# A two-layer block on one core: expert weights, router, x2 and h as two fp16 parts in place of two fp32r parts, with weight scales found on chip

## The reference, cut to what matters

```
x = x + attention(layernorm(x), w_qkv, w_out)
x = x + experts(layernorm(x), Wg, Wu, Wd, Wr, temperature)

attention: 16 heads of 16, rotary q and k, q = elu(q*s)+1, k = elu(k*s)+1,
           kv += k v^T, ks += k, out_t = (q kv) / max(q ks, 1e-6), out @ w_out
experts:   gate = einsum('btd,edi->beti', x, Wg)       # E = 8, D = 256, I = 256
           up   = einsum('btd,edi->beti', x, Wu)
           h    = silu(gate) * up
           e_out = einsum('beti,eid->betd', h, Wd)
           out  = einsum('bte,betd->btd', weights, e_out)
weights:   inh = sigmoid(x @ Wr / temperature); exp(-|inh - 1/e| / 0.1) inside a zone,
           else the two nearest experts; normalised to sum 1
```

## Time and profile before

| | before |
|---|---|
| median of 3 runs | 807.97 us |
| profiled execution, span from first to last instruction | 806.5 us |
| TensorE busy | 760.2 us (94%), 6660 matmuls |
| VectorE busy | 603.2 us (75%) |
| ScalarE busy | 465.4 us (58%) |
| GpSimd busy | 484.7 us (60%) |
| mean granted TensorE clock | 0.968 of full |
| device memory read, written | 16.13 MB, 4.19 MB |

### The profile page before, as it was taken

The page is one execution under the profiler, slowest core; times in us unless marked ns, Lnnn a source line. Parts: engine busy times, 40 slices in busy tenths (PEclk is TensorE's granted clock), DMA queues, the critical chain, the costliest instruction groups (busy, mean ns, idle before and its releaser), DMA issues.

```text
span 806.5 us, 18062 instructions
## 1 busy us (share of the span) xinstructions
PE 760.2 (94%) x6660; PEld 654.1 (81%) x6660; DVE 603.2 (75%) x1596; ACT 465.4 (58%) x886; POOL 484.7 (60%) x538
## 2 busy tenths in 40 slices
PE   4475899999999999999999999999999999999997
PEld 2364688888888888888888888888888888888886
DVE  6788797878877797778877797787877787765433
ACT  3664776666566656666666556657665566534221
POOL 3785678765666665655666666566666555653232
PEclk9676799999999999999999999999999999999999
DMA  4544124122211123122101221121111121100000
GB/s 139 127 103 110 41 78 93 40 43 68 40 28 24 34 66 41 41 43 54 41 20 35 43 66 40 41 43 27 41 40 40 41 53 28 27 1 27 1 1 27
DMA packets 97319, 38.27 MB, mean 47 GB/s; under 512 B 74192, under 2 KB 96976, under 8 KB 97232
## 3 DMA queue, kind: packets, MB, share of 16 engines
q1 hardware_dynamic: 90704, 30.83, 18.1%
q10 hardware_dynamic: 6528, 6.29, 2.7%
HBM read 16.13 MB, written 4.19 MB: 25 GB/s over the span
## 4 chain that ended last, share of the span: by engine, by line
PE 88%; DVE 5%; POOL 2%; ACT 2%; issue 1%; DMA 1%; SPq 0%; DVEq 0%; ACTq 0%; POOLq 0%
PE y L446 22%; PE gate L413 22%; PE up L413 21%; PE front L288 5%; PE back L333 3%; PE front L289 3%; PE back L369 2%; PE back L344 2%; PE up L381 1%; PE front L311 1%; PE front L394 1%; PE back L326 1%; PE back L356 1%; POOL a_lo L1131 1%; PE back L311 1%
## 5 line engine op out<-in xcount | busy, mean ns | idle before, releaser
L1159 POOL TENSOR_TENSOR h_lo<-work,h_hi 128x512 fp32r<-128x512 f32 x128 | 166.3, 1299 | 66.0 <-ACT h_hi L640 66.0
L1131 POOL TENSOR_TENSOR a_lo<-am,a_hi 128x512 f16<-128x512 f32 x120 | 144.6, 1206 | 54.9 <-ACT a_hi L568 52.3
L446 PE MATMUL y<-wd_hi,h_hi 128*128 128x256 f32 x512 | 148.1, 289 | 1.7 <-DVE xa L1032 1.7
L446 PE MATMUL y<-wd_lo,h_hi 128*128 128x256 f32 x512 | 143.9, 281 | 0.0
L446 PE MATMUL y<-wd_hi,h_lo 128*128 128x256 f32 x512 | 143.8, 281 | 0.0
L1020 DVE TENSOR_TENSOR work<-work,up 128x512 f32<-128x512 f32 x128 | 87.1, 680 | 72.1 <-PE up L413 71.7
L640 ACT ACTIVATE h_hi<-work 128x512 fp32r<-128x512 f32 x128 | 80.6, 630 | 64.5 <-DVE work L1020 39.4
L1032 DVE SCALAR_TENSOR_TENSOR xa<-y,wo,xa 128x256 f32<-128x256 f32 x256 | 113.5, 470 | 4.5 <-PE y L446 4.5
L446 PEld LDWEIGHTS y<-wd_hi,h_hi 128*128 128x128 f32 x512 | 96.5, 189 | 4.9 <-issue 2.1
L446 PEld LDWEIGHTS y<-wd_lo,h_hi 128*128 128x128 f32 x512 | 96.4, 188 | 3.1
L446 PEld LDWEIGHTS y<-wd_hi,h_lo 128*128 128x128 f32 x512 | 96.4, 188 | 0.0
(11 more groups left out here) (200 smaller groups left out, 1722.2 us busy)
## 6 DMA issues: line engine op xcount, KB each, us to landing
xr<-xT SPq DMA_DIRECT2D x32, 128.0 KB, 2.5
xa<-x SPq DMA_DIRECT2D x32, 128.0 KB, 2.7
out<-xa SPq DMA_DIRECT2D x32, 128.0 KB, 1.7
xa<-Wg ACTq DMA_DIRECT2D x8, 256.0 KB, 2.9
work<-Wd ACTq DMA_DIRECT2D x8, 256.0 KB, 2.9
work<-Wu ACTq DMA_DIRECT2D x8, 256.0 KB, 2.8
work<-w_qkv SPq DMA_DIRECT2D x2, 384.0 KB, 3.7
qT<-q_st SPq DMA_TRANSPOSE x32, 3.2
```

Source lines behind the costliest of these rows:

```text
L446: m = pe.matmul(Y[t // 2][:, t % 2 * D:(t % 2 + 1) * D], h_p[hi][:, n % 2, t * P:(t + 1) * P], wd_p[wi][:, u // KI, u % KI, :], start=(n % ...
L1131: pool.tensor_tensor(a_p[1][:, heads(r), :], am_place(g, r).rearrange("p (h n) -> p h n", h=4), a_p[0][:, heads(r), :], ALU.subtract).then ...
L1159: pool.tensor_tensor(h_p[1][:, n % 2, :], hb[:, n % 2, :], h_p[0][:, n % 2, :].bitcast(F32), ALU.subtract).then_inc(s_hlo, 1)
```

## The change

- `wr_s`, `wg_p`, `wu_p`, `wd_p`, `x2` and `h_p` become F16. qkv, the output projection and their operands stay fp32r.
- fp16 has a narrow range, so each weight slab (and Wr) is multiplied by a power of two found on chip: ScalarE squares the slab with a running sum (`squares`), TensorE adds over the partitions (`totals`, a matmul with ones), VectorE keeps that sum (`totals_kept`), GpSimd takes its power -1/2 (`inv_norm`), VectorE keeps the exponent bits (`scale`). Five rounds cover the slabs: 0 to 2 with Wr, 3 to 5, 6 to 8, 9 to 11, 12 to 23.
- For Wd slabs, hi and lo are made with the scale inside the instruction. For Wg and Wu slabs, VectorE first multiplies the raw slab in place (`scaled`).
- The scale is taken out again in silu (scale of the gate), in `h_up` (which becomes a scalar_tensor_tensor), in the routing weights (`wn`, one more VectorE instruction per block) and in the router's temperature. `unscale` computes those factors in two parts.
- All 24 raw slabs stay in SBUF; there is no ring. Their loads move from ScalarE's queue to SP's: three after the small loads, then five behind each step's transposes.
- Slabs 12 to 23 are prepared at s = 6, 7 and 8, one step later than before. The head's lists are rewritten around the new steps.

```diff
-        wg_p = [sb(f"wg_{s}", [P, E, KD, I], F32R) for s in ("hi", "lo")]
+        wg_p = [sb(f"wg_{s}", [P, E, KD, I], F16) for s in ("hi", "lo")]
...
+        raw = sb("raw", [P, SLABS, KD, I])
...
-        x2 = [sb(f"x2_{s}", [P, 2, KD, B], F32R) for s in ("hi", "lo")]
+        x2 = [sb(f"x2_{s}", [P, 2, KD, B], F16) for s in ("hi", "lo")]
...
-        h_p = [sb(f"h_{s}", [P, 2, B], F32R) for s in ("hi", "lo")]
+        h_p = [sb(f"h_{s}", [P, 2, B], F16) for s in ("hi", "lo")]
...
-            n = HEAD_SLABS + STEP_SLABS * (s - LAG) + i
-            return n if i < STEP_SLABS and n < SLABS else None
+            n = HEAD_SLABS + STEP_SLABS * (s - LAG - 1) + i
+            return n if s > LAG and i < STEP_SLABS and n < SLABS else None
...
+            def totals(i):
+                cols = batch_cols(i)
+                w.wait_ge(s_onem, 1)
+                w.wait_ge(s_sq, cols.stop)
...
+                pe.matmul(total_bank(i)[:, cols], ones[:, :], ssq[:, cols], start=True, stop=True).then_inc(s_tot, 1)
...
+            def squares(n):
+                _, dst, e_ = slabs[n]
+                w.wait_ge(slab_in[n // 3], 48)
+                act.activation(dst[1][:, e_, :, :], raw[:, n, :, :], ACT.Square,
+                               accum_out=ssq[:, 1 + n:2 + n]).then_inc(s_sq, 1)
...
-                act.activation(dst[0][:, e_, :, :], ring[n % NSL], ACT.Copy).then_inc(s_slab_hi, 1)
-                load_slab(n + NSL - 1)
+                if slab_lo_done(n)[0] is s_slab_lov:
+                    w.wait_ge(slab_in[n // 3], 48)
+                    w.wait_ge(s_sc, batch_of(n) + 1)
+                    act.activation(dst[0][:, e_, :, :], raw[:, n, :, :], ACT.Copy, scale=slab_scale(n)).then_inc(s_slab_hi, 1)
+                else:
+                    w.wait_ge(s_scaled, n - n // 3 + 1)
+                    act.activation(dst[0][:, e_, :, :], raw[:, n, :, :], ACT.Copy).then_inc(s_slab_hi, 1)
...
-                act.activation(hb[:, n % 2, :], G[:, :], ACT.Silu).then_inc(s_g, 1)
+                act.activation(hb[:, n % 2, :], G[:, :], ACT.Silu, scale=isc[:, 1 + 3 * e_:2 + 3 * e_]).then_inc(s_g, 1)
...
+            def totals_kept(i):
+                cols = batch_cols(i)
+                w.wait_ge(s_tot, i + 1)
+                v.tensor_scalar(tb[:, cols], total_bank(i)[:, cols], W_TOP ** -2, 1e-36, ALU.mult,
+                                ALU.max).then_inc(s_tb, 1)
+            def scale(i):
+                cols = batch_cols(i)
+                w.wait_ge(s_pw, i + 1)
+                v.tensor_scalar(sc[:, cols].bitcast(I32), pw[:, cols].bitcast(I32), EXPONENT, None,
+                                ALU.bitwise_and).then_inc(s_sc, 1)
+            def scaled(n):
...
+                w.wait_ge(s_sc, batch_of(n) + 1)
+                v.tensor_scalar(raw[:, n, :, :], raw[:, n, :, :], slab_scale(n), None, ALU.mult).then_inc(s_scaled, 1)
...
-                v.tensor_tensor(hb[:, n % 2, :], hb[:, n % 2, :], U[:, :], ALU.mult).then_inc(s_h, 1)
+                v.scalar_tensor_tensor(out=hb[:, n % 2, :], in0=U[:, :], scalar=ch[:, e_:e_ + 1], in1=hb[:, n % 2, :],
+                                       op0=ALU.mult, op1=ALU.mult).then_inc(s_h, 1)
...
+            def inv_norm(i):
...
+                pool.tensor_tensor(pw[:, cols], tb[:, cols], mhalf[:, 0:1].broadcast_to([P, cols.stop - cols.start]),
+                                   ALU.pow).then_inc(s_pw, 1)
...
+            for n in range(3):
+                load_slab(n)
             for s in range(STEPS):
                 load_xr(s + 2)
                 transpose_q(s); transpose_k(s)
+                for n in range(5 * s + 3, 5 * s + 8):
+                    load_slab(n)
```

Steps whose place in the lists the prediction speaks of, after the change (head, ScalarE, VectorE and GpSimd, and the step s = 5):

```diff
+            exp(4); s2(2); a_hi(3, 2); a_hi(3, 3); q_hi(4); k_hi(4); slab_hi(6); v1(4); slab_hi(7); squares(12)
+            x2_hi(2); slab_hi(8); squares(13); o_hi(3); squares(14); squares(15); s1(3); s2(3); v2(4); slab_hi(9)
+            squares(16); slab_hi(10); squares(17); squares(18); slab_hi(11); a_hi(4, 0); squares(19); x2_hi(3)
+            a_hi(4, 1); squares(20); squares(21); squares(22); squares(23)
...
+            a_lo(3, 0); a_lo(3, 1); s3(2); slab_lo(4); a_lo(3, 2); a_lo(3, 3); slab_lo(6); rstd2_pow(2); v_rest(4)
...
+                if s == LAG:
+                    totals_kept(HEAD_BATCHES)
+                o_sum(c, 0)
+                if s == LAG:
+                    scale(HEAD_BATCHES); unscale(1)
```

More of the change, by code:

```diff
@@ L161, in build @@
         y_out = [sem(f"stored_y{i}") for i in range(4)]
-        slab_in = [sem(f"landed_slab{i}") for i in range(NSL)]
+        slab_in = [sem(f"landed_expert{e}") for e in range(E)]
+        s_onem, s_sq, s_tot, s_tb, s_pw, s_sc, s_scaled, s_isc, s_ch, s_uy, s_unscale = (
+            sem(n) for n in ("ones_m", "squares", "totals", "totals_kept", "inv_norm", "scale", "scaled", "inv_scale", "h_scale",
+                             "y_scale", "unscale"))
         (s_ones, s_mhalf, s_mone, s_rtemp, s_rtemp2, s_id0, s_mask0, s_id, s_mask, s_iota_i, s_iota, s_zvx,
@@ L452, in tensor_program @@
             colmean()
[L454 to L457, removed]
+            qkv(0); qkv(1); totals(0); scores(0, 0); scores(0, 1); qkv(2); av(0); state(0); scores(1, 0); o_T(0)
+            totals(1); scores(1, 1); qkv(3); proj(0); av(1); scores(2, 0); state(1); x2_T(0); totals(2); scores(2, 1)
+            o_T(1); qkv(4); proj(1); av(2); state(2); x2_T(1); scores(3, 0); o_T(2); totals(3); scores(3, 1); proj(2)
+            av(3); x2_T(2); o_T(3); state(3); proj(3); scores(4, 0); scores(4, 1); x2_T(3)
             for s in range(LAG, STEPS):
@@ L648, in scalar_program @@
[L648 to L652 removed]
+            x_hi(0); wqkv_hi(0); wqkv_hi(1)
@@ L1045, in vector_program @@
+            scale(0); k_lo(0); scaled(0); scaled(1); rope(1); x_lo(2); phi(1); tcos_scale(2); q_lo(1); mask(0, 0); mask(0, 1); k_lo(1)
+            mask(0, 2); slab_lo(2); mask(0, 3); cos(2); o_sum(0, 0); bn(4); o_sum(0, 1); rope(2); den_max(0)
             tcos_scale(3); den_rec(0); mask(1, 0); phi(2); norm(0); st_add(0); mask(1, 1); x_lo(3); q_lo(2)
-            mask(1, 2); k_lo(2); mean_var(4); var_eps(4); mask(1, 3); o_lo(0); slab_lo(5); cos(3); x1_add(0); bn2(0)
-            mean_var2(0); o_sum(1, 0); var_eps2(0); o_sum(1, 1); bn(5); mask(2, 0); st_add(1); den_max(1); ln2(0)
@@ L1053, in vector_program @@
-            norm(3); x_lo(5); x2_lo(2); o_lo(3); st_add(3); x1_add(3); bn2(3); mean_var2(3); var_eps2(3); mask(4, 0)
-            ln2(3); mask(4, 1); var_eps(5); x2_lo(3); slab_lo(11)
+            totals_kept(1); mask(1, 2); k_lo(2); mean_var(4); var_eps(4); mask(1, 3); o_lo(0); cos(3); x1_add(0); bn2(0)
+            mean_var2(0); o_sum(1, 0); var_eps2(0); o_sum(1, 1); scale(1); bn(5); scaled(3); mask(2, 0); st_add(1); den_max(1)
+            ln2(0); scaled(4); rope(3); mask(2, 1); den_rec(1); mean_var(5); norm(1); x_lo(4); phi(3); x2_lo(0); totals_kept(2)
@@ new lines, in vector_program @@
+            mask(2, 2); mask(2, 3); q_lo(3); tcos_scale(4); o_lo(1); k_lo(3); cos(4); x1_add(1); bn2(1); mean_var2(1); var_eps2(1)
+            o_sum(2, 0); o_sum(2, 1); ln2(1); den_max(2); slab_lo(5); den_rec(2); st_add(2); wr_lo()
+            norm(2); scale(2); scaled(6); mask(3, 0); mask(3, 1); x2_lo(1); scaled(7); rope(4); o_lo(2); totals_kept(3); mask(3, 2); mask(3, 3); phi(4)
+            x1_add(2); bn2(2); mean_var2(2); var_eps2(2); k_lo(4); q_lo(4); o_sum(3, 0); o_sum(3, 1); ln2(2); den_max(3)
@@ L1055, in vector_program @@
+            den_rec(3); norm(3); x_lo(5); slab_lo(8); x2_lo(2); scale(3); scaled(9); o_lo(3); st_add(3); x1_add(3)
+            bn2(3); scaled(10); mean_var2(3); var_eps2(3); mask(4, 0); ln2(3); mask(4, 1); var_eps(5); unscale(0); rtemp_half()
+            x2_lo(3); slab_lo(11)
             for s in range(LAG, STEPS):
```

170 lines of the change are left out of this document (112 added, 58 removed).

## The result

The changed kernel takes 819.74 us (median of 4 runs, 819.08 to 820.64) against 808.03 us: ratio 1.015, 95% interval 1.0135 to 1.0165. It is slower by 11.7 us where 23.4 us less were forecast, and it lies above the range (769 to 814). The profiled execution's span is 818.1 us at a mean granted clock of 0.948 (before: 806.5 and 0.968).

What follows compares the result with a forecast made beforehand. The prediction took a latency-bound head of nearly 100 us, then TensorE's stream, as the bounds. 806.5 - 35.6 (stream) + 12.2 (head) = 783.1, plus 1.5 to the median: 784.6 us, range 769 to 814.

Steps and rivals of the forecast that it cites:

- wn, 8 in all: nothing: Router on VectorE: one more instruction per block, 8 in all, priced at nothing.
- I leave its length: h_up, behind o_lo on VectorE, becomes a scalar_tensor_tensor; its 0.68 us was taken as unchanged.
- The slack goes to 0.07 us and is not used up: Before proj in each step: the 0.54 us between o_lo's end and proj shrinks by 0.47, without delaying TensorE.
- Stream: TensorE's expert and router matmuls: pitches fall to 216.0 and 109.4 ns, -35.6 us in sum.
- SP's queue, +3: Head: slab issues on SP stand ahead of xr(3), xr(4) and xa(4), +3 us (0 to 10).
- VectorE's eight `scaled`, +3.5 with the small ones: Head: eight multiplies (4.8 us) and sixteen small instructions (2.7), about half in idle time, +3.5 us (1 to 7.5).
- The norms: Head: slab squares and copies on ScalarE +2 us, small VectorE instructions, and a scale round before the first experts +1.5.
- Slabs one step later, +2: Two steps after the first experts: slabs 12 to 23 come later, up needs slab 22's lo part, +2 us (0 to 4).
- GpSimd's slab_lo(4), +1.2: Head: it stands between a_lo(3,1) and a_lo(3,2), for which TensorE waits before av(3), +1.2 us.
- back, -1: Head: slab issues leave ScalarE's queue where it is on the chain, -1 us (0 to -3).
- the pitch isn't the type's: Rival on TensorE's stream: fp16 gains 0 while the head's 12 us are added, 820 us; chance 0.17.
- VectorE's chain becomes the period: Rival: in 27 full steps VectorE's chain gives back at most 0.5 us each, 13.5 in all, 798 us; chance 0.13.

Runs made afterwards that it cites:

- the ladder: Successive cuts from the changed kernel: constant scale 813.4 us, no slab multiplies 805.4, slabs in old steps 801.45, other SP order 793.39, no scale-undoing operations 783.37.
- experiment 5: The kernel before with every fp32r operand as fp16, qkv and proj too, and no scales: 772.95 us, ratio 0.957.
- types-only kernel: The kernel before with fp16 for experts, router, x2 and h, no scale or norm, same lists: 780.53 us, ratio 0.9666.
- the ladder's bottom: Changed kernel with constant scale, no raw-slab multiplies, slabs in old steps, and xr, xa issued ahead of the five slabs on SP: 793.39 us, ratio 0.9819.
- the ladder's end: The 793.39 us kernel (constant scale, no multiplies, old slab steps, other SP order) also without the three scale-undoing operations: 783.37 us, ratio 0.9701.
- experiment 4: The changed kernel with the scale a constant 1024, without squares, totals or pow: 813.4 us, ratio 1.0075.

## Why the prediction was wrong

The forecast was -35.6 and +12.2; the runs show -27.4 and +39.2. The terms of the loss are the steps of the ladder, so each holds its interplay with those still in place. Two steps of the prediction failed. The larger: the work that undoes the scale was put at nothing ("wn, 8 in all: nothing", "I leave its length"), and costs 10.0 to 11.7 us. The second: "The slack goes to 0.07 us and is not used up". It is used up, and TensorE waits for o_lo in front of proj in every step. The head's terms had the right places, but SP's and that of the multiplies were far too small.

- **Stream: the pitch was right, the sum was not.** 215 and 109 ns were measured for 216.0 and 109.4. The sum failed at the slack. The working had 0.54 us of it and 0.47 to lose. But proj never starts less than 0.054 us behind o_lo in any of these steps, and TensorE's part between qkv and proj shrank by 0.50 us only because it stood there: without waits it would have been about 0.64, as y behind av and gate behind `state` also lost the 0.085 and 0.09 us that they took beyond their like before (experiment 5). 0.54 - 0.055 - 0.64 is -0.16 us, which is the wait of 0.16 that the types-only kernel has. The rows of before held both numbers. The Trainium skill's gap of N/2.4 + 2.5 ns ("TensorE: Matmul & The Clock Gate", section "Back-to-back issue gap") agrees with the measured pitch; its sustained figure near 131 ns doesn't show.
- **"wn, 8 in all: nothing"** is the costliest single error: 8.0 us (9.4 on moving it), forecast 0. I priced it by the small ones of the earlier trace rows, 0.17 us, which are instructions that happened to fall beside an idle GpSimd or don't meet it. Its place is where VectorE's list has no room: h_up(n+3) right behind it, `up` waiting for that. The trace of before had the warning, as q_w, a small instruction of the same router step, takes 0.95 to 1.01 us in seven of eight blocks there. The Trainium skill states a rule for it: by "SBUF — State Buffer", section "Who interferes with whom", a VectorE instruction with two SBUF inputs contends with a GpSimd instruction that reads SBUF, one in a 2-port mode contends with GpSimd too, and whichever was issued first holds the shared ports for the whole instruction. The ends of the three instructions above agree, within 0.05 us. It was the rule that spoke against this change, and I didn't weigh it.
- **"I leave its length"**: h_up's 64 ns more and Silu's 88 cost 2.1 and 2.3 us. The Trainium skill ("ScalarE: Activation LUTs", section "What ACT_TABLE_LOAD costs") gives some 93 ns for each operand that is a pointer to one value per partition; 88 was measured.
- **SP's queue, +3**: 8.1 at the ladder's bottom, 4.9 alone. The issues (0.47 to 0.57 us each) were counted; not counted was that xa(5), and with it VectorE's list and then ScalarE's, hangs behind the same five issues.
- **VectorE's eight `scaled`, +3.5 with the small ones**: the multiplies alone 8.0 for all sixteen, and eight of the sixteen stand behind the first gate, where none was priced. The duration was about right for the head: the first eight take 5.1 us for the 4.8 forecast, six at 0.47 to 0.49 and two longer, 0.89 and 1.33. The Trainium skill's double rate ("VectorE: DVE Perf Modes", section "The perf-mode tier table") agrees with the 0.47 us, as a tensor_tensor of 512 columns takes 0.68; the 2 us less that the prediction drew from it did not come. Three of the eight behind the gate take 1.0 to 1.4 us.
- **The norms**, in pieces of ScalarE +2, the small VectorE ones and the first expert step +1.5: 6.3, some 1.5 over the sum of these pieces. At the first gate it is 3.5. The step with the first experts came out nearly as forecast: o_T waits 4.52 us in the whole change and 2.76 with a constant scale, so the round costs 1.8 there. Its price was under-read, as pow on GpSimd takes 2.28 us on 12 columns, not the 0.55 of one column:

```profile
111.78 2.28 POOL L1199 TENSOR_TENSOR pw<-tb,mhalf 128x12 f32<-128x12 f32 x1 [0.64 <-DVE tb L760]
...
116.84 0.42 DVE L954 SCALAR_TENSOR_TENSOR nat<-osb,rec 128x256 f32<-128x256 f32 x1
117.32 0.69 PE L405 MATMUL back<-ident,nat 128*128 128x128 f32 x2 [4.52 <-DVE nat L954]
```

- **Slabs one step later, +2**: the mechanism was right to the instruction (the wait for wu_lo, 2.83 us at 195.96). 4.0 was measured between the medians and 2.5 between the profiled executions. Nothing in the forecast counted what a wait does to the clock, up to 1.3 us where the half clock follows.
- **GpSimd's slab_lo(4), +1.2, and back, -1**: not seen singly; the 2.8 us left at the ladder's end contain both.

The rivals: 820 for "the pitch isn't the type's" hit the time by luck and is false in its mechanism, as the pitch was gained. "VectorE's chain becomes the period" is true, at proj in every step and at `up` in the router steps, which were its two signs. Its price, 13.5 us at most for 27 steps, is of the size of the 8 us by which the gain of the types fell short; it had no part for what scaling costs. The first gate moved by 17 us, inside the 3 to 20 set as the bounds of being wrong, but far above the 6 to 10 that the sum took.

## What to carry to other kernels

Where TensorE is the bound and its waits are near zero, price every added instruction on another engine by the room at its place in that engine's list, and price it as it runs beside GpSimd: 0.2 us of work was 1.08 us and cost 8 us in eight places. When TensorE's stream gets shorter, subtract all that gets shorter from the slack of the next chain, and look at the gap between the end of that chain and TensorE's start afterwards, since waits of 0.2 us in every step stand in no list of long waits. A matmul whose successor comes late costs time only if the gap in front of it isn't shorter by as much.

## What the runs showed of the hardware

- The first fp32r matmul behind 16-bit ones takes 0.085 us (256 columns, y behind av) or 0.09 (512, gate behind `state`) more than its like in the kernel before, and 0.10 (256) at proj in the changed one. At qkv the gap behind it is 0.19 us longer and the one in front 0.19 shorter.
- After waits of 4.5 and 2.8 us the granted clock was 0.50 and 0.53 for about 3 us of full work; in experiment 4 a wait of 2.83 us was followed by 1.00.
- pow on GpSimd: 0.55 us on one column, 0.87 on three, 2.28 on twelve.
- Small VectorE instructions end with the GpSimd instruction that they meet: wn 1.01 to 1.08 us in place of 0.19.

```profile
L1199 POOL TENSOR_TENSOR pw<-tb,mhalf 128x3 f32<-128x3 f32 x3 | 2.6, 865 | 0.0
```
